# Half-tile tails, merged cross scores and new turns in a two-layer decoder kernel

## The chip, the cores and the metric

The kernel runs on one core of a Trainium2 chip. The metric is the time of one execution in microseconds (us), as the device takes it. TensorE (PE in the profile) multiplies, VectorE (DVE), ScalarE (ACT) and GpSimd (POOL) work on tiles, and SyncE (SP) issues DMAs.

## The reference, cut to what matters

Two decoder layers over x of 8 batches, 256 tokens and 256 features. Each layer is self attention, cross attention over 77 context tokens, and a mixture of experts, and each of the three ends in a residual and a layer norm.

```python
x = _layernorm(x + _L0_attn_ref(x, ...))        # gated linear attention, 4 heads
x = _layernorm(x + _L0_xattn_ref(x, ctx_768, ...))  # cross attention, 16 heads of 16
x = _layernorm(x + _L0_ffn_ref(x, ...))         # 8 experts, the best 2 of each token
x = _layernorm(x + _L1_attn_ref(x, ...))        # window of 128 to either side, 16 heads
x = _layernorm(x + _L1_xattn_ref(x, ctx_768, ...))  # cross attention, scores clipped
x = _layernorm(x + _L1_ffn_ref(x, ...))         # 8 experts with a capacity
```

Cross attention in the reference is

```python
att = jax.nn.softmax(jnp.einsum('blhd,bmhd->blmh', q, k) * scale, axis=2)
out = jnp.einsum('blmh,bmhd->blhd', att, v).reshape(b, l, d)
return jnp.einsum('bld,ed->ble', out, Wo) + bo
```

## The kernel before

The batches go in four pairs. Within a pair one batch is p0 and one is p1; each has its own buffers and four of the eight PSUM banks, so that one works while the other waits. What follows calls them layer 1 (the stages that `first_layer` lists: gated linear attention and cross attention X0) and layer 2 (`second_layer`: self attention S1 and cross attention X1). The experts stand between the layers and at the end, and don't take part in the change, apart from the early routing that is mixed into the last pair of each layer.

The work of a batch is a thread, a list of stages. A stage is a small function on one engine: `scores` on TensorE, `max` on VectorE, `exp` on ScalarE and so on. `in_turns` merges the threads of p0 and p1 into one list: it takes so many stages of p0, then so many of p1, by the numbers in `TURNS0`, `LAST0`, `TURNS1`, `LAST1` and `TURNS_HEAD`. `play` lets every engine walk through that one list and issue the stages that it owns. So each engine does its own stages in the order of the list, strictly one behind the other, and between engines only semaphores hold. Stages of different engines that stand side by side in a thread overlap; what matters is the order of the stages of one engine.

Attention goes in these steps. `scores` multiplies queries by keys (lines 1583 and 1591), `max` takes the negated row maxima (L874, L878), `split` turns them into bf16 (L886 to L890), `nmT` and `nmTe` turn them (L1604, L635). `ST` computes the scores again, transposed (L1630), and adds the maxima as shift rows (L1612); in X1, `clip` (L895) stands between the two and `shift` adds the rows. `exp` is on ScalarE (L645). Then comes the tail: `values` (L1658), `OT` copies the result (L649), `untr` turns it back (L1666), `norm` divides by the sums (L901, L903), `tout` turns it (L1673), `onT` copies it (L653), `wo` is the output product (L1680), and `res` adds the residual and starts the layer norm (L910, L833 to L840), whose power is on GpSimd (L1388). `final` is L846. A tail handles both 128-token tiles of the batch at once. In gated linear attention the last stages are `g_turn` (L1775), which needs the rows that GpSimd and ScalarE scaled, `g_yT` (L710), `g_wo` (L1783), `g_res` (L976) and `g_fin`.

A float32 product of one call leaves two matmul records in the trace. In cross scores a call has 77 columns, one head's keys; 16 calls, 32 records, make a unit of 128 queries, and four of them run in different row groups of the array.

`idle` (L1566) issues bf16 products that nobody reads, in counts given by the `IDLE` constants: 4 before the shift rows of p0's cross attention, 4 of 204 columns after p1's first unit of scores, 4 and 6 after the products that wait for a clip, 4 in p1's `g_turn` and 2 in each `route` of the pairs before the last. Outside the pairs are 50 before layer 2, 20 and 8 around the last experts, and 12 in each layer's last `turn_result`.

TensorE's order in a middle pair of layer 1, from the mix on:

```
g_mix:0 g_mix:1 k:0 g_turn:0 g_turn:1 g_wo:0 g_wo:1 k:1 v:0 turn:0 v:1 q:0 turn:1 q:1 scores.0:0 scores.0:1
scores.1:0 scores.1:1 nmT:0 ST.0:0 nmT:1 ST.0:1 ST.1:0 ST.1:1 values:0 values:1 untr:0 untr:1 tout:0 tout:1 wo:0 wo:1
```

(The number after the colon is the batch, p0 or p1.) VectorE's has `g_res:0 g_fin:0 g_res:1 g_fin:1`.

## Time and profile before

| what | us |
|---|---|
| median of 3 runs | 1130.51 |
| lowest and highest run | 1126.09, 1133.84 |
| the profiled execution's span, first to last instruction | 1131.2 |
| TensorE busy | 1010.0 (89%) |
| VectorE busy | 618.1 (55%) |
| ScalarE busy | 425.0 (38%) |
| GpSimd busy | 255.4 (23%) |

The profile gives the profiled execution by its span, and no time beside it; the span lies within the times of the runs. Layer 1's pairs fill the span from the start to some 380 us, the first experts follow to some 600, layer 2's pairs to some 1035, and the last experts end it. Busy shares are means over all of that.

### The profile page before, as it was taken

To read this page: it belongs to the slowest core of one execution; us is meant where nothing else is said; L and a number is where in the kernel's file an instruction comes from. 1 tells how busy PE (TensorE), PEld (TensorE's weight loads), DVE (VectorE), ACT (ScalarE), POOL (GpSimd) and SP (SyncE) were. 2 spreads that over 40 slices of the span, in tenths; PEclk is the share of its full clock that TensorE was granted. 3 is DMA by queue.
4 is the path that set the end of the run, shared out by engine and by line. 5 is a ranking of instruction groups with operands and counts; after the bars stand their busy time and mean duration, and the time that the engine had idled before them with its cause. 6 is when DMAs were issued, how large, how long until landed. Compare 5 with 4: busy or idle time off the path is not lost.

```text
span 1131.2 us, 20802 instructions
## 1 busy us (share of the span) xinstructions
PE 1010.0 (89%) x8612; PEld 719.1 (64%) x8612; DVE 618.1 (55%) x1398; ACT 425.0 (38%) x557; POOL 255.4 (23%) x282
## 2 busy tenths in 40 slices
PE   6889889999987899999998798879888987986997
PEld 3666566576575799997445465747565665654566
DVE  2653753662667564333334846675575668765443
ACT  1533533524433355555541254142416231541112
POOL 0310310120130233333322020231013110210662
PEclk9999999899897899999999899999999999997999
DMA  6013413211400691111113000200020010004447
GB/s 188 1 43 126 135 43 107 89 43 44 152 1 1 254 378 57 47 48 47 43 39 98 1 2 6 85 2 5 1 76 2 6 38 1 1 2 131 130 135 236
DMA packets 64237, 80.50 MB, mean 71 GB/s; under 512 B 12736, under 2 KB 57680, under 8 KB 63120
## 3 DMA queue, kind: packets, MB, share of 16 engines
q1 hardware_dynamic: 53392, 61.15, 16.3%
q0 software_dynamic: 5664, 15.47, 4.2%
q10 hardware_dynamic: 5088, 2.56, 0.9%
q8 instruction: 68, 1.11, 0.4%
q14 instruction: 25, 0.20, 0.1%
HBM read 46.13 MB, written 33.03 MB: 70 GB/s over the span
## 4 chain that ended last, share of the span: by engine, by line
PE 61%; DVE 17%; ACT 12%; issue 5%; DMA 2%; POOL 2%; SPq 0%; ACTq 0%; DVEq 0%; POOLq 0%
PE ps L1522 8%; PE ps L1857 7%; DVE sb_arena L874 6%; ACT sb_arena L645 6%; PE ps L1658 5%; PE ps L1680 4%; PE ps L1885 4%; PE ps L1868 3%; PE ps L1728 3%; PE ps L1783 3%; DVE sb_arena L878 3%; PE ps L1566 2%; PE ps L1995 2%; PE ps L1630 2%; PE ps L1905 2%
## 5 line engine op out<-in xcount | busy, mean ns | idle before, releaser
L645 ACT ACTIVATE sb_arena<-ps 77x2048 f32<-77x2048 f32 (+1 forms) x64 | 116.5, 1880 | 27.9 <-PE ps L1612 26.7
L1388 POOL TENSOR_TENSOR sb_arena<-sb_arena,sb_neghalf 128x2 f32<-128x2 f32 x40 | 28.7, 719 | 397.2 <-DVE sb_arena L840 397.2
L1522 PE MATMUL ps<-sb_arena,sb_wreg 128*128 128x256 f32 (+1 forms) x512 | 110.8, 365 | 6.8 <-issue 3.8
L1522 PEld LDWEIGHTS ps<-sb_arena,sb_wreg 128*128 128x128 f32 (+1 forms) x512 | 89.0, 195 | 23.7 <-issue 8.3
L1857 PE MATMUL ps<-sb_arena 128*128 128x128 f32 x800 | 100.2, 280 | 3.2 <-ACT sb_arena L757 2.3
L1630 PE MATMUL ps<-sb_arena 32*77 32x256 f32 (+1 forms) x1024 | 78.4, 424 | 25.8 <-ACT sb_arena L645 13.1
L1857 PEld LDWEIGHTS ps<-sb_arena 128*128 128x128 f32 x800 | 97.0, 196 | 5.2 <-ACT sb_arena L757 2.9
L757 ACT ACTIVATE sb_arena<-sb_arena 128x1024 f32 x72 | 76.0, 1057 | 16.8 <-issue 12.4
L1630 PEld LDWEIGHTS ps<-sb_arena 32*77 32x77 f32 (+1 forms) x1024 | 44.3, 177 | 46.1 <-ACT sb_arena L645 24.2
L874 DVE TENSOR_REDUCE sb_arena<-ps 128x8 f32<-128x2048 f32 x32 | 71.0, 2282 | 3.5 <-PE ps L1586 3.5
L1566 PE MATMUL ps<-sb_headrow,sb_identb 128*32 128x512 bf16 (+1 forms) x266 | 65.8, 385 | 1.4 <-DVE sb_arena L878 1.3
L1465 POOL DMA_INDIRECT outs<-sb_arena,sb_idx x36 | 35.5, 987 | 134.8 <-ACT sb_arena L743 134.8
L901 DVE RECIPROCAL sb_arena<-ps 128x32 f32<-128x32 f32 x24 | 8.6, 357 | 100.2 <-PE ps L1666 98.7
L635 ACT ACTIVATE sb_nmTb<-ps 128x256 bf16<-128x256 f32 x24 | 9.2, 383 | 143.5 <-PE ps L1604 143.5
L1658 PE MATMUL ps<-sb_arena,sb_va 77*32 77x256 f32 (+1 forms) x1024 | 58.5, 381 | 3.1 <-ACT sb_arena L645 2.5
L1728 PE MATMUL ps<-sb_wreg,sb_arena 128*128 128x512 f32 x128 | 60.7, 635 | 0.2 <-DVE sb_arena L926 0.2
L1409 POOL TENSOR_SCALAR_AFFINE_SELECT sb_arena<-sb_arena 128x512 f32<-128x512 f32 x48 | 29.6, 647 | 125.2 <-ACT sb_arena L645 125.2
L878 DVE TENSOR_REDUCE sb_arena<-ps 128x16 f32<-128x1232 f32 x32 | 45.4, 1438 | 21.1 <-PE ps L1591 21.0
L846 DVE TENSOR_SCALAR sb_arena<-sb_arena 128x256 f32<-128x256 f32 x80 | 39.2, 531 | 27.3 <-POOL sb_arena L1388 27.1
L1680 PE MATMUL ps<-sb_wreg,sb_arena 128*128 128x256 f32 x192 | 45.2, 384 | 5.7 <-ACT sb_arena L653 5.7
L1658 PEld LDWEIGHTS ps<-sb_arena,sb_va 77*32 77x32 f32 (+1 forms) x1024 | 31.2, 110 | 27.4 <-ACT sb_arena L645 8.7
L1583 PE MATMUL ps<-sb_arena 32*128 32x256 f32 x512 | 36.7, 400 | 13.2 <-DVE sb_arena L874 13.2
(285 smaller groups left out, 1886.9 us busy)
## 6 DMA issues: line engine op xcount, KB each, us to landing
sb_arena<-in_m_w SPq DMA_DIRECT2D x8, 1536.0 KB, 9.8
sent<-sb_xres SPq DMA_DIRECT2D x32, 256.0 KB, 2.6
sb_arena<-outs SPq DMA_DIRECT2D x16, 512.0 KB, 6.0
outs<-sb_zeros SPq DMA_DIRECT2D x4, 1664.0 KB, 9.7
sent<-sb_zeros SPq DMA_DIRECT2D x2, 2560.0 KB, 13.7
sb_arena<-in_m_w SPq DMA_DIRECT2D x16, 256.0 KB, 3.4
early<-sb_xres SPq DMA_DIRECT2D x12, 256.0 KB, 2.9
sb_arena<-in_xT SPq DMA_DIRECT2D x8, 256.0 KB, 3.2
```

Source lines behind the costliest of these rows:

```text
L645: nc.scalar.activation(dst, src, ACT.Exp).then_inc(S(f"h_PT{p}"), 1)
L757: nc.scalar.activation(arena[:, to:to + 1024], arena[:, bass.ds(blk * WORDS + 1024 * part, 1024)], ACT.Copy).then_inc(S(signal), 1)
L874: v.tensor_reduce(b.nm[:, :, u].rearrange("p (t r) -> p r t", t=NT), bank(p, 0, RT).rearrange("p r (t k) -> p r t k", t=NT), axis=AX.X, op ...
L878: v.tensor_reduce(b.nm[:, u * RT:(u + 1) * RT, :], bank(p, 0, RT)[:, :, 0:G * M].rearrange("p r (g k) -> p r g k", g=G), axis=AX.X, op=ALU ...
L1522: ins = mm(dst[:, m * cols:(m + 1) * cols], wt[0:rows, k, m * P:(m + 1) * P], src[0:rows, k, 0:cols], start=(k == 0), stop=(k == KC - 1))
L1566: ins = mm(bank(p, n)[IDLE:P, first:], identb[:, IDLE:P], headrow[:, :, :].rearrange("p g k -> p (g k)")[:, first:], start=True, stop=True ...
L1630: ins = mm(bank(p, r)[0:c.keys, a * L:(a + 1) * L], key, b.q[rows_of(r), u // 2 if c.selfattn else u, :], start=(a == 0), stop=False, skip ...
L1658: ins = mm(bank(p, 2 + g // 2)[rows_of(r), (g % 2) * L:(g % 2 + 1) * L], b.va[0:c.keys, kt, g * RT + r, :], b.PT[0:c.keys, g, first:first ...
L1680: ins = mm(bank(p, 3)[:, t * D:(t + 1) * D], bufs[p].onT[:, k, t * P:(t + 1) * P], W[f"{c.name}_wo"][:, k, :], start=(k == 0), stop=(k == ...
L1728: ins = mm(bank(p, 2 + t), b.xT[:, k, t * P:(t + 1) * P], W[wt][:, k, :], start=(k == 0), stop=(k == KC - 1))
L1857: ins = mm(to[:, m * P:(m + 1) * P], w[:, k, m * P:(m + 1) * P], slots0[j % 2].xT[:, k, :], start=(k == 0), stop=(k == KC - 1))
L1885: ins = mm(to[rows, :], slots0[j % 2].xT[:, k, rows], weights_of(c, blk, at + FH * k, FH, at + FH * k), start=(k == 0), stop=(k == KC - 1) ...
```

## The change

1. Tails in halves. `values` and `OT` are stages for two of the four head groups each; `untr`, `norm`, `tout`, `onT`, `wo` and `res` are stages for one 128-token tile each. The second tile's turned heads and its result go to banks of their own (`turned_bank`, `result_bank`).
2. Cross scores. One call multiplies 128 queries by the keys of two heads, 154 columns, so a unit has 8 calls in place of 16.
3. The unread products in the pairs go (six counts are 0). The 50, 20, 12 and 8 remain; the 12 of p0 now wait for its residual.
4. One list of turns for each layer in place of a list for each pair. In layer 1 every turn is one stage. In layer 2 it is a new list of some 500 numbers. The places of the early routing in the last pair change with it.
5. The early count moves from p0's bank to p1's, with its waits.

TensorE's order in a middle pair of layer 1 becomes

```
g_mix:0 g_mix:1 k:0 g_turn:1 g_turn:0 g_wo:1 g_wo:0 k:1 v:0 v:1 turn:0 turn:1 q:0 q:1 scores.0:0 scores.0:1
scores.1:0 scores.1:1 nmT:0 nmT:1 ST.0:0 ST.0:1 ST.1:0 ST.1:1 values.0:0 values.0:1 values.1:0 values.1:1
untr.0:0 untr.0:1 untr.1:0 untr.1:1 tout.0:0 tout.0:1 tout.1:0 tout.1:1 wo.0:0 wo.0:1 wo.1:0 wo.1:1
```

and VectorE's has `g_res:0 g_res:1 g_fin:0 g_fin:1`. In layer 2 the middle pairs keep the order of before but for neighbours that change places; the tail of S1 becomes

```
values.0:0 values.1:0 values.0:1 values.1:1 untr.0:0 untr.1:0 untr.0:1 tout.0:0 untr.1:1 tout.1:0 tout.0:1 wo.0:0 wo.1:0 tout.1:1 wo.0:1 wo.1:1
```

```diff
-IDLE, IDLE_SPLIT, IDLE_CLIP = 96, 4, (4, 6)
-IDLE_TURN, IDLE_LAYERS, IDLE_ROWS, IDLE_SCORES, IDLE_RESULT, IDLE_MIXED, IDLE_ROUTE = 4, 50, 20, 4, 12, 8, 2
+IDLE, IDLE_SPLIT, IDLE_CLIP = 96, 0, (0, 0)
+IDLE_TURN, IDLE_LAYERS, IDLE_ROWS, IDLE_SCORES, IDLE_RESULT, IDLE_MIXED, IDLE_ROUTE = 0, 50, 20, 0, 12, 8, 0
...
-    for t in range(NT):
-        out += [("scores", c, t), ("max", c, t)]
+    for i in range(c.score_units):
+        out += [("scores", c, i), ("max", c, i)]
...
-    return [(n, c) for n in ("values", "OT", "untr", "norm", "tout", "onT", "wo", "res", "rstd", "final")]
+    out = []
+    for i in range(2):
+        out += [("values", c, i), ("OT", c, i)]
+    for n in (("untr", "norm"), ("tout", "onT"), ("wo", "res")):
+        for t in range(NT):
+            out += [(x, c, t) for x in n]
+    return out + [("rstd", c), ("final", c)]
...
-def in_turns(n, threads, turns, extra):
+def in_turns(threads, turns, extra):
 
     out, at = [], [0, 0]
     for i, count in enumerate(turns):
         p = i % 2
-        for stage, m in threads[p][at[p]:at[p] + count]:
-            if m < PAIRS:
-                out.append((stage, p, m))
-            out += [((e,), 0, n) for e in extra.get((p, *stage), [])]
+        for stage, n in threads[p][at[p]:at[p] + count]:
+            out.append((stage, p, n))
+            out += [((e,), 0, n) for e in extra.get((p, n, *stage), [])]
         at[p] += count
-    assert at == [len(t) for t in threads]
+    assert at == [len(t) for t in threads], (at, [len(t) for t in threads])
...
-TURNS0 = (3, 3, 4, 2, 3, 4, 2, 3, 4, 2, 3, 4, 5, 7, 4, 1, 2, 4, 4, 4, 2, 1, 4, 4, 1, 2, 2, 2, 2, 2, 2, 2, 2, 1, 2, 7, 6, 3, 5, 4)
-TURNS1 = (3, 3, 2, 2, 1, 1, 2, 2, 5, 5, 5, 5, 2, 2, 2, 2, 2, 2, 3, 3, 2, 1, 3, 4, 1, 5, 6, 2, 2, 3, 3, 2, 3, 1, 3, 5, 3, 3, 1, 1, 3, 3, 2, 1, 2, 3, 8, 3, 3, 5, 4, 7, 4, 4)
-LAST0 = (2, 2, 2, 2, 6, 6, 2, 2, 3, 2, 6, 5, 5, 1, 2, 1, 3, 8, 3, 1, 2, 5, 5, 6, 2, 2, 3, 2, 2, 2, 7, 5, 4, 7, 3, 3)
-LAST1 = (3, 3, 2, 2, 2, 2, 1, 1, 5, 5, 5, 4, 1, 2, 2, 2, 2, 2, 1, 1, 3, 3, 6, 1, 1, 4, 2, 1, 2, 2, 2, 3, 4, 4, 1, 1, 4, 3, 1, 4, 3, 3, 2, 2, 2, 2, 2, 1, 1, 2, 3, 2, 3, 4, 6, 6, 8, 8)
-TURNS_HEAD = (3, 2, 3, 3, 2, 1, 1, 2, 2, 3)
+TURNS0 = (1,) * 560
+TURNS1 = (4, 2, 1, 1, 4, 1, 1, 1, 1, 6, 1, 1, 1, 1, 1, 1, 2, 2, 1, 1, 2, 2, 5, 1, 1, 3, 2, 2, 1, 2, 1, 1, 1, 1, 1, 1, 1, 2, 2, 2, 3, 2, 1, 1, 2, 1,
...
+def whole_thread(head, thread, p):
+
+    return head + [(stage, m) for n in range(PAIRS) for stage, m in thread(p, n) if m < PAIRS]
...
+EXTRA0 = {(1, LAST, "g_sp"): ["choose"], (1, LAST, "g_mix"): ["count"], (1, LAST, "g_y"): ["counts", "rank"],
+          (1, LAST, "split", X0): ["hots", "table"], (0, LAST, "tout", X0, 1): ["place"], (0, LAST, "onT", X0, 1): ["raw"],
+          (0, LAST, "wo", X0, 1): ["turned"], (1, LAST, "norm", X0, 1): ["index"], (0, LAST, "rstd", X0): ["first"],
+          (1, LAST, "final", X0): ["blocks"], (1, LAST, "store"): ["gather"]}
+EXTRA1 = {(0, 3, "kz", S1): ["choose"], (1, 3, "va", S1): ["count", "counts"], (0, 3, "values", S1, 0): ["rank"], (0, 3, "values", S1, 1): ["hots"],
+          (0, 3, "rstd", X1): ["place"]}
...
+    head = of_pair(0, "g_keys", "g_low", "g_decay", "g_z")
+    return in_turns([whole_thread(head, first_thread, p) for p in range(2)], TURNS0, EXTRA0)
...
+        def turned_bank(p, t):
+
+            return bank(p, 1 if t else 2)[:, 0:KC * P].rearrange("p (k q) -> p k q", k=KC)
+
+        def result_bank(p, t):
+
+            return bank(p, 2 if t else 3)[:, 0:D]
...
-            sp.wait_ge(S("h_res0"), X0.at(PAIRS))
+            sp.wait_ge(S("h_res0"), NT * X0.at(PAIRS))
...
-            def heads(p, n, c):
-                act.wait_ge(S(f"h_OT_done{p}"), c.at(n) + 1)
-                nc.scalar.activation(bufs[p].OT, bank(p, 2, 2), ACT.Copy).then_inc(S(f"h_OT{p}"), 1)
-
-            def onT(p, n, c):
-                act.wait_ge(S(f"h_onT_done{p}"), c.at(n) + 1)
-                nc.scalar.activation(bufs[p].onT, halves(bank(p, 2)), ACT.Copy).then_inc(S(f"h_onT{p}"), 1)
+            def heads(p, n, c, i):
+                act.wait_ge(S(f"h_OT_done{p}"), 2 * c.at(n) + i + 1)
+                nc.scalar.activation(bufs[p].OT[:, 2 * i:2 * i + 2, :], halves(bank(p, 2 + i)), ACT.Copy).then_inc(S(f"h_OT{p}"), 1)
+
+            def onT(p, n, c, t):
+                rows = slice(t * P, (t + 1) * P)
+                act.wait_ge(S(f"h_onT_done{p}"), NT * c.at(n) + t + 1)
+                nc.scalar.activation(bufs[p].onT[:, :, rows], turned_bank(p, t), ACT.Copy).then_inc(S(f"h_onT{p}"), 1)
...
+            def norm(p, n, c, t):
+                b = bufs[p]
+                dve.wait_ge(S(f"h_O{p}"), NT * c.at(n) + t + 1)
+                o = bank(p, t).rearrange("p (h x) -> p h x", x=2 * DH)
+                v.reciprocal(b.rec[:, t, :], o[:, :, DH]).then_inc(S(f"h_on{p}"), 1)
+                dve.wait_ge(S(f"h_on{p}"), 2 * (NT * c.at(n) + t) + 1)
+                v.tensor_tensor(b.on[:, t, :].rearrange("p (h x) -> p h x", h=H), o[:, :, 0:DH],
+                                b.rec[:, t, :].unsqueeze(2).broadcast_to([P, H, DH]), ALU.mult).then_inc(S(f"h_on{p}"), 1)
+
+            def residual(p, n, c, t):
+                b = bufs[p]
+                dve.wait_ge(S(f"h_wo{p}"), NT * c.at(n) + t + 1)
+                if t == 0:
+                    dve.wait_ge(S(f"h_xb{p}"), c.at(n) + 1)
+                v.tensor_tensor(b.res[:, t, :], result_bank(p, t), b.xb[:, t, :], ALU.add).then_inc(S(f"h_res{p}"), 1)
+                dve.wait_ge(S(f"h_res{p}"), NT * c.at(n) + t + 1)
+                ins = v.bn_stats(b.st1 if t else b.st0, b.res[:, t, :])
+                if t + 1 == NT:
+                    ins.then_inc(S(f"h_moments{p}"), 1)
+                    moments("h", p, c.at(n))
...
-                    for g in range(G):
+                    for k in range(KC):
                         for r in range(RT):
-                            ins = mm(bank(p, r)[:, g * M:(g + 1) * M], b.q[rows_of(r), g // 2, u * P:(u + 1) * P], kz[rows_of(r), g // 2, g % 2, :],
-                                     start=(g == 0), stop=True, skip_group_check=True)
-                    if p == 1 and u == 0:
-                        ins = idle(p, IDLE_SCORES, 0, G * M)
+                            ins = mm(bank(p, r)[:, 2 * k * M:2 * (k + 1) * M], b.q[rows_of(r), k, u * P:(u + 1) * P],
+                                     kz[rows_of(r), k, :, :].rearrange("p a m -> p (a m)"), start=(k == 0), stop=True, skip_group_check=True)
...
+            def values(p, n, c, i):
+                b = bufs[p]
+                if i == 0:
+                    pe.wait_ge(S(f"h_PT{p}"), c.exps_at(n) + c.exp_units)
+                for g in (2 * i, 2 * i + 1):
...
+            def untranspose(p, n, c, t):
+                if t == 0:
+                    pe.wait_ge(S(f"h_OT{p}"), 2 * (c.at(n) + 1))
+                for g in range(G):
+                    ins = tr(bank(p, t)[:, g * P:(g + 1) * P], bufs[p].OT[:, g, t * P:(t + 1) * P], ident[:, :])
...
+            def turn_out(p, n, c, t):
+                pe.wait_ge(S(f"h_on{p}"), 2 * (NT * c.at(n) + t + 1))
                 for k in range(KC):
-                    for t in range(NT):
-                        ins = tr(bank(p, 2)[:, k * L + t * P:k * L + (t + 1) * P], bufs[p].on[:, t, k * P:(k + 1) * P], ident[:, :])
+                    ins = tr(turned_bank(p, t)[:, k, :], bufs[p].on[:, t, k * P:(k + 1) * P], ident[:, :])
...
+            def project_out(p, n, c, t):
+                pe.wait_ge(S(f"h_onT{p}"), NT * c.at(n) + t + 1)
+                for k in range(KC):
+                    ins = mm(result_bank(p, t), bufs[p].onT[:, k, t * P:(t + 1) * P], W[f"{c.name}_wo"][:, k, :],
+                             start=(k == 0), stop=(k == KC - 1))
...
             def turn_result(p, n, c):
                 if n + 1 == PAIRS and p == 0:
+                    pe.wait_ge(S(f"h_res{p}"), NT * (c.at(n) + 1))
...
             def gla_keys(p, n):
                 b = bufs[p]
                 pe.wait_ge(S(f"a_in{p}"), 64 * (n + 1))
+                if n:
+                    pe.wait_ge(S(f"h_res{p}"), NT * X0.at(n))
```

## Rows read from the trace of the kernel before

**Rows 1.** The page, chain that ended last, by engine

```profile
PE 61%; DVE 17%; ACT 12%; issue 5%; DMA 2%; POOL 2%; SPq 0%; ACTq 0%; DVEq 0%; POOLq 0%
```

**Rows 2.** Windows of core 0: start:end, length, busy PE PEld DVE ACT POOL, clock, DMA, GB/s

```profile
111.36:198.10 86.74, 79.35 (x646) 56.39 (x646) 44.24 (x90) 35.31 (x52) 15.56 (x14) 1.00 0.31 100
...
730.70:833.94 103.24, 90.09 (x1024) 62.31 (x1024) 64.65 (x112) 36.84 (x40) 17.68 (x24) 1.00 0.08 23
...
785.60:805.40 19.80, 17.07 (x261) 9.24 (x263) 14.90 (x10) 7.32 (x8) 0.00 (x0) 1.00 0.01 2
...
135.35:142.04 6.69, 4.24 (x30) 2.99 (x29) 3.66 (x4) 4.49 (x10) 5.27 (x4) 1.00 0.00 0
```

**Rows 3.** The same window, the unread products of line 1566 alone

```profile
785.60:805.40 19.80, 6.57 (x28) 2.20 (x28) 1.00 0.01 2
```

**Rows 4.** Timeline of TensorE, layer 1: start, duration, line, tiles, count, wait

```profile
140.94 1.09 PE L1775 MATMUL ps<-sb_ident,sb_arena 128*128 128x128 f32 x8 [0.80 <-POOL sb_arena L1456]
...
142.04 7.20 PE L1783 MATMUL ps<-sb_wreg,sb_arena 128*128 128x256 f32 x32
...
149.08 1.01 PE L1522 MATMUL ps<-sb_arena,sb_wreg 96*128 96x77 f32 x8
...
157.12 2.13 PE L1591 MATMUL ps<-sb_arena 32*128 32x77 f32 x64
...
179.22 3.63 PE L1680 MATMUL ps<-sb_wreg,sb_arena 128*128 128x256 f32 x16
...
194.81 0.60 PE L1566 MATMUL ps<-sb_headrow,sb_identb 128*32 128x512 bf16 x2
```

**Rows 5.** Timeline of VectorE, the same pair

```profile
145.81 0.69 DVE L976 TENSOR_TENSOR sb_arena<-ps,sb_arena 128x512 f32<-128x512 f32 x1 [6.63 <-PE ps L1783]
...
147.61 0.17 DVE L840 TENSOR_SCALAR sb_arena<-sb_arena 128x2 f32<-128x2 f32 x1
...
158.32 4.21 DVE L878 TENSOR_REDUCE sb_arena<-ps 128x16 f32<-128x1232 f32 x3 [1.99 <-PE ps L1591]
```

**Rows 6.** Timeline of ScalarE, the same pair

```profile
140.98 2.11 ACT L710 ACTIVATE sb_arena<-ps 128x1024 f32<-128x1024 f32 x2
...
166.18 7.15 ACT L645 ACTIVATE sb_arena<-ps 77x2048 f32<-77x2048 f32 x4
```

**Rows 7.** Timeline of TensorE, layer 2

```profile
785.65 2.13 PE L1591 MATMUL ps<-sb_arena 32*128 32x77 f32 x64
...
791.12 1.04 PE L1566 MATMUL ps<-sb_headrow,sb_identb 128*32 128x512 bf16 x4 [0.22 <-DVE sb_arena L878]
...
792.85 1.10 PE L1630 MATMUL ps<-sb_arena 32*77 32x256 f32 x16 [0.47 <-ACT sb_nmTb L635]
...
802.96 0.42 PE L1612 MATMUL ps<-sb_nmTb,sb_headrow 32*77 32x256 bf16 x8
...
812.63 1.99 PE L1680 MATMUL ps<-sb_wreg,sb_arena 128*128 128x256 f32 x8 [0.69 <-ACT sb_arena L653]
...
816.23 1.99 PE L1680 MATMUL ps<-sb_wreg,sb_arena 128*128 128x256 f32 x8 [0.74 <-ACT sb_arena L653]
```

**Rows 8.** Timeline of VectorE, layer 2, the clips

```profile
794.02 4.49 DVE L895 TENSOR_SCALAR ps<-ps 77x2048 f32<-77x2048 f32 x2 [1.18 <-PE ps L1630]
...
800.21 4.49 DVE L895 TENSOR_SCALAR ps<-ps 77x2048 f32<-77x2048 f32 x2 [1.70 <-PE ps L1630]
```

**Rows 9.** Windows of core 0 at a lower clock

```profile
346.00:348.00 2.00, 2.00 (x16) 0.76 (x12) 1.39 (x1) 0.00 (x0) 0.00 (x0) 0.50 0.00 0
...
644.00:646.00 2.00, 1.56 (x16) 1.36 (x20) 1.93 (x6) 1.97 (x3) 0.00 (x0) 0.64 0.00 0
```

**Rows 10.** Timeline of TensorE in the window of 346

```profile
349.16 2.00 PE L1630 MATMUL ps<-sb_arena 32*77 32x256 f32 x16 [0.47 <-ACT sb_nmTb L635]
```

**Rows 11.** Timeline of TensorE, the early choice in layer 2

```profile
933.16 0.43 PE L1797 MATMUL ps<-sb_masked,sb_causal 128*128 128x96 f32 x2 [1.10 <-DVE sb_masked L1036]
```

**Rows 12.** Timeline of VectorE, p0's last residual in layer 1

```profile
371.42 0.68 DVE L910 TENSOR_TENSOR sb_arena<-ps,sb_arena 128x512 f32<-128x512 f32 x1
```

More of the change, by code:

```diff
@@ L207, in second_thread, with second_layer @@
         of_pair(n + 1, *self_head(S1)[3:])
-def second_head():
-    return in_turns(0, [of_pair(0, "mix", "mix_rstd", "mix_fin", *self_head(S1))] * 2, TURNS_HEAD, {})
-def second_layer(n):
-    extra = {}
-    if n + 1 == PAIRS:
-        extra = {(1, "exp", S1, 0): ["rank", "hots"], (1, "wo", X1): ["place"]}
-    if n + 2 == PAIRS:
-        extra = {(1, "kz", S1): ["choose"], (0, "v", S1): ["count", "counts"]}
-    return in_turns(n, [second_thread(p, n) for p in range(2)], LAST1 if n + 1 == PAIRS else TURNS1, extra)
+def second_layer():
+    head = of_pair(0, "mix", "mix_rstd", "mix_fin", *self_head(S1))
+    return in_turns([whole_thread(head, second_thread, p) for p in range(2)], TURNS1, EXTRA1)
 def play(order, stages):
@@ L777, in _ @@
             act.wait_ge(S("rescaled"), 3)
-            play(head1, stages)
-            for order in order1:
-                play(order, second)
+            play(order1, second)
             picks(3, 4)
@@ L1309, in _ @@
             scale_bias(["s1_bq", "x1_bq"], "rescaled")
-            play(head1, stages)
-            for order in order1:
-                play(order, stages | routing(1))
+            play(order1, stages | routing(1))
             choose_late(1)
@@ L1475, in store1 @@
                     unread(p)
-            play(head1, stages)
-            for order in order1:
-                play(order, stages | {"store": lambda p, n: store1(p, n)})
+            play(order1, stages | {"store": lambda p, n: store1(p, n)})
             def gather1(e):
```

108 lines of the change are left out of this document (36 added, 72 removed), and 9 rows, old and new, of the table TURNS1.

## Prediction

> **What bounds the kernel now.** I read the chain that ended last first: TensorE holds 61% of it, VectorE 17%, ScalarE 12% [rows 1]. The windows then show how full TensorE is. One pair of batches takes 86.7 us in layer 1 and 103.2 us in layer 2, and TensorE has no matmul for 7.4 and 13.2 us of them (span of the window less TensorE's busy time) [rows 2]. So a saving counts only where TensorE, or the engine that it waits for, comes last. The timelines by engine show four kinds of stretch: the dense ones, where TensorE sets the pace; the maxima and the clips, where VectorE does (a clip takes 2.25 us, four stand in a pair [rows 8]); the exponentials, where ScalarE does (1.8 us each [rows 6]); and the joints between them, where the hand-written order decides.
>
> The last view is the windows with the granted clock. In the maxima and clips of cross attention, 785.6 to 805.4, TensorE is busy for 17.07 of 19.8 us at full clock [rows 2], but 6.57 us of that are unread products [rows 3]. The reader should keep both numbers.
>
> The profiled span is 1131.2 us; the median of the runs is 1130.5. I carry the sum on the span and take the 0.7 off at the end.
>
> **Layer 2, a pair at full clock.** Laid side by side engine by engine, the new order has nearly the old sequence: the two batches still alternate, p0 slightly ahead. New are the halves.
> - Self attention's tail. TensorE waits some 0.6 us there for the normalisation of the second batch, as in cross attention; with halves the other tile's turns fill that. -0.6 us.
> - Merged score product. 64 records of 77 columns take 2.13 us, about 1.03 us for a unit of 32 [rows 7]. A unit becomes 16 records of 154 columns. The floor is half, 0.5 us; the ceiling is no saving, if a record costs by its columns. Sixteen records of 256 columns take about 1.0 us [rows 7], 60 ns each against 32 ns for 77 columns; on the line between them 154 columns cost 44 ns, 0.7 us a unit. Only the first unit lies on the path, since VectorE needs 1.4 us for each maximum [rows 5]. -0.3 us (0 to -0.5).
> - Split idle. Four unread products start at 791.12, when p0's last maximum is there, and the shift rows must wait 0.97 us for them [rows 7]. What they are to cover is one small cast, some 0.2 us by the 0.17 us of a small operation [rows 5]. -0.75 us.
> - Clip idles. The second pair of clips starts at 800.21 and its first half ends at 802.45 [rows 8], but the shift rows start at 802.96 [rows 7], behind four unread products: 0.45 us. At the first clip I estimate 0.2. -0.65 us.
> - Cross attention's tail. TensorE waits 0.69 and 0.74 us for ScalarE's copy of the turned heads [rows 7]. In halves, one tile's turn hides the other's copy. A tail gets five more operations on ScalarE and VectorE, each at least the 0.17 us of a small one [rows 5]; both engines are idle beside it. -1.1 us.
>
> The Trainium skill, TensorEngine Tiling (Array Packing), section Instruction Overhead, says that a matmul has some 60 cycles of overhead and is no cheaper below 60 columns. By it both 77 and 154 columns lie above the floor, a unit would take what it took, and 0.3 us would be lost again in each of eight cross attentions, 2.4 us in all. The rows speak against it: 256 columns cost less than twice what 77 cost.
>
> Together -3.4 us, -10.2 for three pairs. The last pair has no follow-up work in its tail, and its 12 unread products now wait for the residual: -2.6. Its early routing sits better: choosing the experts makes TensorE wait 1.10 us between two value products [rows 11], and in the new order all projections run during that chain: -1.0. The head of the layer: -0.5, as the first batch's query product fills the wait for the second batch. **Layer 2: -14.3 us** (-9 to -18).
>
> **Layer 1, a pair at full clock.** Here the strict turns move work across the joints.
> - After the gated mix p1's turn now comes ahead of p0's (the key product stands before it in p0's thread). TensorE still waits there for GpSimd's rows of p1, until 140.94 [rows 4]. Then come p1's turn, p0's turn, and p1's output product waits for ScalarE's 1.0 us copy of p1's turned rows, which starts at about 142.1. Today p0's copy runs from 140.98 [rows 6] and the product starts at 142.04 [rows 4]. It now starts at 143.2: +1.1 us.
> - VectorE's order changes from residual p0, final p0, residual p1, final p1 to both residuals, then both finals, and p0's residual comes behind the second output product. A residual with its statistics takes 1.97 us, 145.81 to 147.78 [rows 5]. The second product ends 7.0 us after the start of the first, at 150.2 [rows 4]; p0's input is normalised at 150.2 + 1.97 + 1.9 + 0.75 = 154.9. TensorE has one key and two value products in between, some 0.87 us each, to 152.8: it waits 2.1 us. Both queries follow both turns, and the scores start at 160.4 instead of 157.12 [rows 4]: 3.3 us late, the 1.1 included.
> - Maxima to exponentials: -0.3 (merged) and -0.75 (idles), against +1.0, since p0's shift rows now stand behind the last maximum of p1 and behind p1's own rows in all three engines. 0.
> - Tail: the first half of p1's values stands before the second half of p0's and waits for p1's last exponential, 1.8 us less the 0.9 of p0's half [rows 6]. The output products start at 180.1 instead of 179.22 [rows 4]: +0.9.
> - The router's two groups of two unread products lay on a full TensorE, 0.43 us from the start of one to the next work [rows 4]: -0.9.
>
> That is +3.3 us a pair, +9.9 for three. In the last pair VectorE's one-hots and tables hold the chain anyway; only its end counts, where SyncE's queue holds the load of the experts' weights until p0's residual is done. Today that residual runs from 371.42 to 372.1 [rows 12]. In strict turns its second half comes behind four halves of normalisation, the index and two other halves of the residual, and ends at about 373.1: +1.0. **Layer 1: +10.9 us** (+4 to +15). The halves lie beside TensorE's work here too; without that cover 24 tails of five small operations would cost 20 us.
>
> Both layers: 10.9 - 14.3 = -3.4 us.
>
> **The clock.** The unread products do more than fill. Within the paired work I count seven falls to the lower level (0.5, that is 1.2 GHz), each behind thin work on TensorE; two windows of them are shown [rows 9]. The one of 346 lasted 13 us, behind maxima with a wait of 1.5 us, though TensorE was full again in most of it. The one of 644 stands at the joint between maxima and exponentials, and the same joint fell in two of four pairs. At the lower level 16 records of products take 2.00 us instead of 1.10 [rows 7, 10]. Without idles and with merged scores the clip stretch [rows 2] has 17.07 - 6.57 - 1.3 = 9.2 us of work in some 17.5 us, 53%, about what that joint has. So I expect falls in two of the four pairs of layer 2. Each costs two products at +0.9, two groups of shift rows at +0.25 and 1.8 us of the values: 4.1 us, 8.2 in all. In layer 1 the wait before the output product, 4.24 us busy in 6.69 [rows 2] with 1 us of idles in it, should fall in two more pairs, at an estimated 1.2 us each: 2.4. Together +10.6. The Trainium skill, TensorE: Matmul & The Clock Gate, section What's actually happening, calls the lower level the default, which activity releases; the rows agree as far as every fall here follows thin work.
>
> Sum: 1131.2 - 3.4 + 10.6 = 1138.4 on the span, **1137.7 us** against the median.
>
> **The rivals.**
> 1. *The clock holds* (0.28). What is left are matmuls still, and the self scores run warm with half a microsecond of wait in every 2.2. Then 1130.5 - 3.4 = 1127 (1121 to 1132).
> 2. *The clock falls in every thin stretch* (0.22), the slower side: four pairs of layer 2 and three cross attentions of layer 1 at 4.1, four joints at 1.2, 33.5 us less 3.4. It passes 1% with the fourth fall of the 4.1 kind. For it: 53% busy. Against it: two of four at the joint. 1147 to 1161.
> 3. *The strict turns are paid for* (0.12): p0's residual gets through sooner than my row by row sum, and the value half waits less. Then layer 1 costs 4 instead of 10.9 and the clock holds: 1120; 1116 if layer 2 gives its 18.
> 4. *The new order does not act* (0.03): every engine plays its stages from one list, so the order can't fail to take place; only the merged product can save nothing, +2.4.
>
> My forecast (0.35) has 1132 to 1147 as its own range. For 8 in 10 the range takes in rival 1 and the lower half of rival 2: 1118 to 1154.
>
> **Chances.** 1% is 11 us, about what a measurement of this kernel can tell from no change. Below 1119: rival 3 and an edge of rival 1, 0.15. Above 1142: rival 2 and over a third of my case, 0.35. Between them 0.50.
>
> **What would show it.** In a pair of layer 1, a wait of 2 us before the cross attention's input is turned, and a period of 90 instead of 86.7 us. In layer 2, no waits in the tails, clips 1.6 us nearer to the self tail, and periods below 100 us where the clock is 1.00. In the clock's windows, falls in the clip stretch. I am wrong if the clock shows none there, or if the scores of layer 1 start as early as now.

## The result, and the profile after

The changed kernel takes 1171.02 us (median of 4, 1165.77 to 1177.97) against 1129.35 us: ratio 1.0376, 95% interval 1.0327 to 1.0425, slower. Forecast were 1137.7 us and a range to 1154. The profiled execution has a span of 1164.0 us; it was the fastest of the four, so the traces show 32.8 of the some 42 us.

The cores' view has span and mean granted clock of TensorE, first the changed kernel, then the kernel before:

```profile
core 0: 1164.0 us, clock 0.919
```

```profile
core 0: 1131.2 us, clock 0.967
```

At the lower of the two levels, 0.5, TensorE spends an estimated (1 - 0.919) x 2 x 1164.0 = 189 us in place of 75. Its busy time hardly changed (1003.0 and 1010.0 us), although the unread products are gone. The page's line of TensorE and its chain that ended last [rows 1], which gained in TensorE and VectorE:

```profile
PE 1003.0 (86%) x7928; PEld 727.0 (62%) x7928; DVE 628.2 (54%) x1470; ACT 432.2 (37%) x605; POOL 256.7 (22%) x282
...
PE 63%; DVE 19%; ACT 7%; issue 5%; DMA 3%; POOL 2%; SPq 0%; ACTq 0%; DVEq 0%; POOLq 0%
```

The windows of the changed kernel (start:end, length, busy PE, PEld, DVE, ACT, POOL, clock, DMA share, GB/s) answer to [rows 2]: a pair of each layer, the maxima and clips, then the joint from the gated mix to its output product. The last three cut one clip stretch and what follows into the part ahead of a fall, the fall, and the part behind it.

```profile
120.20:215.73 95.53, 81.62 (x567) 59.24 (x566) 44.51 (x96) 35.99 (x56) 15.65 (x14) 0.91 0.28 90
757.19:862.81 105.62, 88.23 (x932) 62.23 (x933) 67.57 (x125) 38.06 (x48) 18.11 (x24) 0.92 0.07 22
811.41:831.31 19.90, 11.33 (x173) 6.41 (x176) 14.93 (x10) 7.76 (x8) 0.00 (x0) 0.85 0.01 2
144.03:152.99 8.96, 4.46 (x25) 4.25 (x25) 3.75 (x4) 4.60 (x10) 5.35 (x4) 0.81 0.00 0
...
819.00:825.00 6.00, 2.82 (x48) 1.42 (x48) 4.58 (x3) 3.43 (x3) 0.00 (x0) 1.00 0.00 0
825.00:842.00 17.00, 14.37 (x117) 8.82 (x118) 6.48 (x9) 7.11 (x8) 0.00 (x0) 0.51 0.01 1
842.00:850.00 8.00, 7.57 (x41) 6.14 (x40) 5.73 (x21) 2.21 (x6) 1.95 (x3) 0.98 0.00 2
```

The reader should see two things. A pair of layer 1 is 8.8 us longer, one of layer 2 is 2.4. And the clip stretch comes first at full clock with TensorE thin (2.82 of 6.0 us busy); then the clock is at 0.51 for 17 us, though TensorE is busy for 14.37 of them.

The timeline of TensorE, layer 1, beside [rows 4]:

```profile
149.71 3.45 PE L1794 MATMUL ps<-sb_ident,sb_arena 128*128 128x128 f32 x16 [3.43 <-POOL sb_arena L1476]
...
164.66 0.66 PE L1534 MATMUL ps<-sb_ident,sb_arena 128*128 128x128 f32 x4 [1.98 <-DVE sb_arena L859]
166.42 1.11 PE L1534 MATMUL ps<-sb_ident,sb_arena 128*128 128x128 f32 x4 [1.11 <-DVE sb_arena L859]
167.32 4.87 PE L1540 MATMUL ps<-sb_arena,sb_wreg 128*128 128x256 f32 x16
...
178.95 0.52 PE L1621 MATMUL ps<-sb_identb,sb_nmb 128*128 128x128 bf16 x4 [2.29 <-DVE sb_nmb L903]
...
189.27 4.37 PE L1676 MATMUL ps<-sb_arena,sb_va 77*32 77x256 f32 x48 [0.69 <-ACT sb_arena L654]
193.57 3.67 PE L1684 MATMUL ps<-sb_ident,sb_arena 128*128 128x128 f32 x16
```

The waits are where the steps put them, 3.43 us before the turns, 1.98 before p0's input (2.1 foreseen), 0.69 in the values. Behind nearly each of them stands work that is longer than its records take at full clock: 16 turns in 3.45 us, 16 in 3.67, where 8 took 1.09 [rows 4].

The same view for layer 2, beside [rows 7]:

```profile
817.53 1.10 PE L1647 MATMUL ps<-sb_arena 32*77 32x256 f32 x16 [0.47 <-ACT sb_nmTb L644]
...
823.25 0.42 PE L1629 MATMUL ps<-sb_nmTb,sb_headrow 32*77 32x256 bf16 x8 [1.78 <-DVE ps L908]
...
825.64 2.00 PE L1647 MATMUL ps<-sb_arena 32*77 32x256 f32 x16 [1.09 <-ACT sb_arena L654]
...
830.65 7.06 PE L1676 MATMUL ps<-sb_arena,sb_va 77*32 77x256 f32 x64
```

From the scores to the second pass of products it is 6.12 us in place of 7.20, the saving of 1.05 that was foreseen. From there to the output product it is 24.43 in place of 19.78: the 64 value records take 7.06 us, and 3.73 at full clock (in a run below).

A landmark parts the loss: VectorE's first maxima of layer 2 start 23.4 us later, by its timeline before and after. The experts took the same: from their first turn to these maxima it is 243.3 us, and 243.7 before. So layer 1 lost 23.4 us, and layer 2 9.4. Foreseen were 13.3 (10.9 + 2.4) and -6.1 (-14.3 + 8.2). (The second line is from a view that ends before the seventh maximum.)

```profile
625.06 15.47 DVE L874 TENSOR_REDUCE sb_arena<-ps 128x8 f32<-128x2048 f32 x7 [0.86 <-PE ps L1586]
```

```profile
648.49 13.28 DVE L887 TENSOR_REDUCE sb_arena<-ps 128x8 f32<-128x2048 f32 x6 [0.86 <-PE ps L1605]
```

### The profile page after: what moved, and what is told of

The parts are those of the page before. It is cut to its first block, busy times and chain, and to the rows that moved or that the text cites. A ratio compares the mean times of both kernels' runs of the same rounds, so it can differ in the third digit from the quotient of the medians.

```text
span 1164.0 us, 19568 instructions
## 1 busy us (share of the span) xinstructions
PE 1003.0 (86%) x7928; PEld 727.0 (62%) x7928; DVE 628.2 (54%) x1470; ACT 432.2 (37%) x605; POOL 256.7 (22%) x282
## 3 DMA queue, kind: packets, MB, share of 16 engines
q8 instruction: 63, 1.03, 0.4%
## 4 chain that ended last, share of the span: by engine, by line
PE 63%; DVE 19%; ACT 7%; issue 5%; DMA 3%; POOL 2%; SPq 0%; ACTq 0%; DVEq 0%; POOLq 0%
PE ps L1540 8%; PE ps L1876 7%; PE ps L1676 6%; DVE sb_arena L887 6%; ACT sb_arena L654 5%; PE ps L1747 5%; PE ps L1904 3%; PE ps L1647 3%; PE ps L1887 3%; DVE sb_arena L891 3%; PE ps L1696 3%; DVE ps L908 3%; PE ps L1802 2%; PE ps L1684 2%; PE ps L2012 2%
## 5 line engine op out<-in xcount | busy, mean ns | idle before, releaser
L1540 PE MATMUL ps<-sb_arena,sb_wreg 128*128 128x256 f32 (+1 forms) x512 | 113.7, 375 | 5.5 <-issue 3.8
L1647 PE MATMUL ps<-sb_arena 32*77 32x256 f32 (+1 forms) x1024 | 88.9, 471 | 21.1 <-ACT sb_arena L654 11.7
L1540 PEld LDWEIGHTS ps<-sb_arena,sb_wreg 128*128 128x128 f32 (+1 forms) x512 | 93.1, 203 | 22.4 <-issue 8.7
L767 ACT ACTIVATE sb_arena<-sb_arena 128x1024 f32 x72 | 76.0, 1057 | 17.9 <-issue 13.9
L1676 PE MATMUL ps<-sb_arena,sb_va 77*32 77x256 f32 (+1 forms) x1024 | 78.2, 471 | 5.1 <-ACT sb_arena L654 4.5
L914 DVE RECIPROCAL sb_arena<-ps 128x16 f32<-128x16 f32 x48 | 12.3, 256 | 125.4 <-PE ps L1684 122.7
L1647 PEld LDWEIGHTS ps<-sb_arena 32*77 32x77 f32 (+1 forms) x1024 | 48.7, 193 | 43.8 <-ACT sb_arena L654 22.8
L1676 PEld LDWEIGHTS ps<-sb_arena,sb_va 77*32 77x32 f32 (+1 forms) x1024 | 38.0, 131 | 39.5 <-issue 16.9
L1747 PE MATMUL ps<-sb_wreg,sb_arena 128*128 128x512 f32 x128 | 55.9, 595 | 0.2 <-DVE sb_arena L944 0.2
L1887 PE MATMUL ps<-sb_arena 128*128 128x256 f32 x200 | 47.4, 380 | 0.0
L633 ACT ACTIVATE sb_arena<-ps 128x512 f32<-128x512 f32 x24 | 14.1, 596 | 89.6 <-PE ps L1534 89.6
## 6 DMA issues: line engine op xcount, KB each, us to landing
sent<-sb_zeros SPq DMA_DIRECT2D x2, 2560.0 KB, 14.3
```

The lines of the kernel that those rows point to most:

```text
L767: nc.scalar.activation(arena[:, to:to + 1024], arena[:, bass.ds(blk * WORDS + 1024 * part, 1024)], ACT.Copy).then_inc(S(signal), 1)
L1540: ins = mm(dst[:, m * cols:(m + 1) * cols], wt[0:rows, k, m * P:(m + 1) * P], src[0:rows, k, 0:cols], start=(k == 0), stop=(k == KC - 1))
L1647: ins = mm(bank(p, r)[0:c.keys, a * L:(a + 1) * L], key, b.q[rows_of(r), u // 2 if c.selfattn else u, :], start=(a == 0), stop=False, skip ...
L1676: ins = mm(bank(p, 2 + i)[rows_of(r), (g % 2) * L:(g % 2 + 1) * L], b.va[0:c.keys, kt, g * RT + r, :], b.PT[0:c.keys, g, first:first + L], ...
L1747: ins = mm(bank(p, 2 + t), b.xT[:, k, t * P:(t + 1) * P], W[wt][:, k, :], start=(k == 0), stop=(k == KC - 1))
L1887: ins = mm(bank(1, 3)[:, 0:D], slots0[p].hT[:, m, :], work["w3"][:, m, :], start=(m == 0), stop=(m == MC - 1))
```

## The experiments

The first four make a square with the two kernels: unread products or none, strict or old turns in layer 1.

```diff
-IDLE, IDLE_SPLIT, IDLE_CLIP = 96, 0, (0, 0)
-IDLE_TURN, ..., IDLE_SCORES, ..., IDLE_ROUTE = 0, ..., 0, ..., 0
+IDLE, IDLE_SPLIT, IDLE_CLIP = 96, 4, (4, 6)
+IDLE_TURN, ..., IDLE_SCORES, ..., IDLE_ROUTE = 4, ..., 4, ..., 2
```

**idles_back** is the changed kernel with this.

> The changed kernel with the six counts of unread products as before (4, (4, 6), 4, 4, 2), everything else changed. Theory, the unread products held the clock: the mean granted clock returns from 0.919 to about 0.965, and only the order and the halves are left. My sum without the clock was -3.4 us, and the unread products on the path were worth 11.3 of gain in it (1.4 in each of four pairs of layer 2, 0.75 and 0.9 in layer 1), so 1130.5 - 3.4 + 11.3 = 1138 us (1133 to 1144). Rival, the halves and the strict turns make the stretches thin by themselves: the falls of the clock stay and the time stays above 1158 us.

1140.47 us (ratio to the kernel before 1.0085, 1.0051 to 1.0118), within the theory's range. The square below shows that luck had a part in it: the strict order costs 25.7 us where the sum has 16.6, the rest of the change gains 15.7 where it has 8.7 (16.6 - 8.7 = 11.3 - 3.4), and the two errors nearly cancel.

**before_no_idles** is the kernel before with the same lines the other way.

> The kernel before with the same six counts at 0, nothing else changed. Theory, the unread products held the clock: they save 11.3 us on the path, and the clock takes back what the changed kernel lost by it, 1171 less 1127 (my sum without the clock) = 44 us: 1130.5 - 11.3 + 44 = 1163 us (1152 to 1172), granted clock about 0.92. Rival, the order and the halves cost the time: the products were in the way, and the time is 1119 to 1135 us with a clock above 0.95.

1165.05 us (1.0295, 1.025 to 1.034), clock 0.906, within the theory's range. The old order with 16 score calls and whole tails loses 35 us by this alone. Its window from the second pass of products to the output product in layer 2:

```profile
807.23:833.31 26.08, 20.66 (x183) 11.69 (x183) 11.78 (x10) 10.51 (x8) 0.00 (x0) 0.57 0.01 1
```

19.78 us with the unread products. So the long fall needs neither halves nor new turns.

**old_order** (no unread products) and **idles_old_order** (with them) give layer 1 the old order of every engine, halves side by side; only the early count keeps its new place:

```diff
-TURNS0 = (1,) * 560
+TURNS0 = (1, 1, 1, 1, 1, 1, 1, 1, 3, 3, 4, 2, 3, 4, 2, 3, 4, 2, 3, 4, 5, 7, 4, 1, 2, 4, 4, 4, 2, 1, 4, 4, 1, 2, 2, 2,
...
```

> The changed kernel without unread products, but TURNS0 is a list that gives layer 1 the order of before, with the two halves of each tail stage side by side. Theory, the order costs what its waits cost and no more: 3.3 us a pair for three pairs, 1171 - 9.9 = 1161 us (1156 to 1167), and the cross attentions of layer 1 show falls of the clock as now. Rival, the waits of the strict order (3.4, 2.0 and 2.3 us in a pair of layer 1) are what brings the clock down: the falls of layer 1 go back to the six of before, another 10 us or more are gained, 1150 us or less.

> Both at once: the six counts of unread products as before, and layer 1 in the order of before. What is left of the change are the halves, the merged score product and the order of layer 2. Theory: 1138 - 9.9 = 1128 us (1122 to 1133), and layer 2 has periods some 2 us shorter than the 103.2 and 105 us of before. Rival, the halves cost time by their extra operations: 1138 us or more.

1146.28 us (1.0148, 1.0107 to 1.019) and 1114.76 us (0.9863, 0.9832 to 0.9894). The theory missed in both: the strict order costs not 10 but 25 us. In the first the rival's number held, but not its mechanism, as is shown below the table.

| us, median | strict turns | old turns | difference |
|---|---|---|---|
| no unread products | 1171.0 | 1146.3 | 24.7 |
| unread products | 1140.5 | 1114.8 | 25.7 |
| difference | 30.5 | 31.5 | |

The two differences add up with hardly anything between them, but the order doesn't cost by the same means in both columns. The estimate of time at the lower level, (1 - clock) x 2 x span, is as a median over each kernel's runs 203 us (strict) and 191 (old) without unread products, 77 and 47 with them. So without them the old order is 24.7 us faster with about as much time at the lower level. Windows of old_order, for a pair of layer 1, from the mix to the first output product, and from there to the scores:

```profile
114.20:206.04 91.84, 82.66 (x566) 58.66 (x566) 44.93 (x96) 35.89 (x56) 15.56 (x14) 0.89 0.29 93
...
140.28:148.02 7.74, 5.21 (x29) 4.50 (x27) 4.02 (x6) 4.49 (x10) 5.35 (x4) 0.68 0.00 0
148.02:163.95 15.93, 15.24 (x73) 12.47 (x73) 8.69 (x28) 2.94 (x5) 3.54 (x4) 0.94 0.24 74
```

In the changed kernel the three are 95.53 us at 0.91, 9.26 at 0.82 and 19.14 at 0.91: longer at a higher clock. TensorE is idle for 13.9 us of that pair (95.53 - 81.62) and for 9.2 of this one. There the order costs by its waits. With unread products, where the old order keeps its clock, the strict one spends 30 us more at the lower level. By the values, 7.06 us for 3.73, work there takes about twice its time, so by this estimate the clock makes up at most 15 of the 25.7 us, and the waits the rest.

The kernel with unread products and the old order, 1114.8 us, is 1.4% faster than the kernel before. Its windows (a pair of layer 2; layer 1 from the mix to the first output product; layer 2 from the second pass of products to the output product) and a line of its timeline of TensorE:

```profile
722.00:822.45 100.45, 88.08 (x960) 60.47 (x961) 67.26 (x125) 37.78 (x48) 18.11 (x24) 1.00 0.08 24
...
136.53:143.60 7.07, 4.62 (x33) 3.18 (x31) 4.01 (x6) 4.49 (x10) 5.35 (x4) 1.00 0.00 0
...
783.11:801.67 18.56, 16.92 (x202) 8.60 (x203) 10.58 (x10) 10.35 (x10) 0.00 (x0) 1.00 0.01 2
```

```profile
795.61 3.73 PE L1681 MATMUL ps<-sb_arena,sb_va 77*32 77x256 f32 x64 [0.18 <-ACT sb_arena L657]
```

**turn_first** and **res_order** put back one part each of the strict order; of TensorE's and VectorE's order in the middle pairs of layer 1 only this changes (in turn_first ScalarE's two copies between turn and product change places too; in the last pair a few stages beside them move):

```
turn_first:  g_turn:1 g_turn:0 g_wo:1 g_wo:0    (for g_turn:0 g_turn:1 g_wo:0 g_wo:1)
res_order:   g_res:0 g_res:1 g_fin:0 g_fin:1    (for g_res:0 g_fin:0 g_res:1 g_fin:1)
```

> From the kernel with unread products and the old order of layer 1 (1114.8 us), one part of the strict turns put back: p1's turn, copy and output product after the gated mix stand ahead of p0's, in all four pairs; VectorE's order is the old one. Theory: p1's product starts 1.1 us later, p0's residual must wait for the second product, and the thin stretch before the product brings the clock down once in a pair (1.2 us): 3.5 to 4.5 us a pair, 1130 us (1124 to 1136). Rival, the strict turns cost by the order of the residuals: 1119 us or less.

> From the same kernel, the other part alone: VectorE does both residuals and then both final steps (with their power on GpSimd), TensorE's turns stay old. Theory: p0's final step comes behind p1's residual, which is 1.2 us later than now, and little of it is covered: 1.2 us a pair, 1120 us (1117 to 1123). Rival, this order is the costly one (the 2.0 and 1.1 us of wait before the two turns in the strict kernel): 1126 us or more.

1142.58 us (1.0125, 1.0079 to 1.017) and 1125.06 us (0.9964, 0.9944 to 0.9985). The first costs 27.8 us, more than either account gave, and as much as all strict turns together. Its windows, from the mix to the first output product and on to the scores, and VectorE's timeline:

```profile
143.96:153.31 9.35, 5.82 (x32) 4.85 (x31) 4.01 (x6) 4.60 (x10) 5.35 (x4) 0.82 0.00 0
153.31:171.47 18.16, 14.75 (x75) 11.60 (x73) 8.64 (x28) 2.94 (x5) 3.54 (x4) 1.00 0.22 65
```

```profile
160.45 0.69 DVE L997 TENSOR_TENSOR sb_arena<-ps,sb_arena 128x512 f32<-128x512 f32 x1 [12.29 <-PE ps L1807]
```

p0's residual waits for the second output product, 12.29 us against 6.63 [rows 5]. That is 3.1 us more from product to scores (18.16 against 15.08), at full clock; the first window is 2.3 longer, with a fall in it. Together 5.4 us in this pair, 22 if all four are alike, and more falls elsewhere. Both this kernel and the strict one put p1's turn ahead and leave p0's residual first; no kernel was run that exchanges the residuals too, so whether it is the combination that costs stays open. In res_order the stretch from product to scores takes 16.19, 1.1 us more, as expected; the four of them are 4.4 of its 10.3 us, which are twice what was expected. The rest goes with the clock, 0.969 in place of 0.979, (0.031 x 1123.9 - 0.021 x 1113.0) x 2 = 23 us more at the lower level. The two parts, 27.8 and 10.3 us, don't add up to the 25.7 of the whole strict order, so neither is a share of it.

**no_clip**, **no_split** and **clip_only** ask which unread products matter. The first two start from idles_old_order, the third from the changed kernel.

```diff
 no_clip:   IDLE_CLIP = (0, 0)
 no_split:  IDLE_SPLIT = 0, IDLE_SCORES = 0
 clip_only: IDLE_CLIP = (4, 6), the other five 0
```

> From the same kernel, the 4 and 6 unread products around each clip left out, the others kept. Theory: these hold the clock in layer 2. Without them the stretch from the clips to the output product takes what it takes in the changed kernel, 24.7 in place of 18.6 us, in four pairs: 1139 us (1130 to 1145). Rival, the 4 products before the shift rows and the 4 in the scores hold it: without those of the clips 0.65 us a pair is saved, 1112 us.

> From the same kernel, the 4 unread products before the shift rows and the 4 after the first score unit left out, those of the clips kept. Theory: they lie on the path and cost 0.75 us in each of eight cross attentions, and the clock stays: 1109 us (1106 to 1112). Rival, they hold the clock as well: 1120 us or more, with falls in the cross attentions of layer 1, which have no others.

> The changed kernel with the 4 and 6 unread products around each clip and no others. Theory: the cross attentions of layer 2 lose the long falls (clips to output product 24.7 us now, 18.6 with all unread products); without those of the scores a short fall stays as in no_split, 21.2: 3.5 us in each of four pairs, 1157 us (1151 to 1162), layer 1 as it is. Rival, layer 2's falls come from the order and the halves: 1166 us or more.

1137.08 us (1.0067, 1.0043 to 1.0092), 1126.89 us (0.9987, 0.9964 to 1.0009) and 1152.58 us (1.0229, 1.0181 to 1.0277). no_clip is the theory's: 22 us for four clip stretches. In no_split the theory fell and the rival held: scores to products is 6.12 us in place of 6.87, the 0.75 that they cost, but the clock takes back more, in layer 1 too (from 163 to 170 us, behind the maxima of cross attention, it is 0.52). clip_only lies in its expected range. Windows from the second pass of products to the output product, no_clip, no_split and clip_only:

```profile
789.40:813.83 24.43, 18.47 (x183) 10.86 (x183) 11.31 (x11) 10.65 (x10) 0.00 (x0) 0.65 0.00 1
```

```profile
788.39:809.67 21.28, 19.73 (x202) 9.39 (x203) 11.31 (x12) 10.31 (x10) 0.00 (x0) 0.85 0.01 2
```

```profile
811.49:832.94 21.45, 19.90 (x202) 9.46 (x203) 11.31 (x12) 10.31 (x10) 0.00 (x0) 0.84 0.00 1
```

With both kinds it is 18.56 us at clock 1.00. So each kind holds a part: without the clips' the clock is low from 797 to the output product (0.50), without the others' it falls at the start of the stretch (0.51 from 788 to 795) and is 1.00 for the rest. clip_only gives 18 of the 30.5 us back, layer 1 as it was.

**single_heads** issues 16 calls of one head again.

> From the kernel with unread products and the old order of layer 1 (1114.8 us), the cross scores again as 16 calls of 77 columns in place of 8 of 154, nothing else. Theory (a record costs by columns only in part): the first unit is on the path, its maxima start 0.3 us later, in eight cross attentions, 1117.2 us (1116 to 1119). Rival, the merged product thins TensorE's work and costs clock: 1113 us or less. Rival from a price by columns alone: 1114.8.

1122.06 us (0.9925, 0.9902 to 0.9948), 7.3 more, above the expected 1116 to 1119. From scores to products it is 7.20 in place of 6.87 us, 0.33 us in each of eight, 2.6: the expected price. A part of the rest is a fall in layer 1's last pair that both the kernel before [rows 9] and this one have, and the merged one hasn't; windows of 13 us of that stretch, single_heads and idles_old_order:

```profile
346.00:359.00 13.00, 10.58 (x108) 5.74 (x104) 11.47 (x54) 4.40 (x4) 0.00 (x0) 0.51 0.01 2
```

```profile
344.00:357.00 13.00, 8.45 (x142) 5.35 (x146) 12.48 (x65) 8.86 (x8) 0.00 (x0) 1.00 0.01 3
```

The merged calls gave TensorE less to do and kept it at full clock there; why, these runs don't tell. That fall isn't the whole rest: from the first scores of the last pair to its last output product it is 33.82 us against 32.00, 1.8 of the 8.6 between the profiled spans. Where the others come from wasn't followed.

**old_layer2** and **old_layer2_b** give layer 2 the order of before too. The first had a wait of my making.

> From the same kernel, TURNS1 is a list that gives layer 2 the order of before too, the two halves of each tail stage side by side (the early routing keeps its new places). What is then left of the change are halves and merged scores. Theory, the interleaved halves and the new places of the last pair gain: 1.0 us a pair and 1.4 more in the last are lost, 1120 us (1117 to 1123). Rival, the halves gain by themselves, in whatever order: 1113 to 1116 us.

> The kernel of old_layer2, but ScalarE copies p0's value halves after p1's last exponential, as before. Theory, the new order of layer 2 is worth something by itself, but little: without that wait the self tail takes 11.0 us or less in place of 13.3, three pairs give back 2.3 each, 1124 to 1126 us; the rest to 1114.8 is order, most of it in the last pair and in falls of the clock. Rival, the halves gain by themselves: 1114 to 1118 us.

1131.98 us (1.0012, 0.9993 to 1.0032) and 1120.86 us (0.9938, 0.9912 to 0.9964). In the first, ScalarE's list had p0's second value half ahead of p1's last exponential (L652 exp, L656 the copy), and TensorE paid:

```profile
767.40 0.60 ACT L656 ACTIVATE sb_arena<-ps 128x512 f32<-128x512 f32 x1 [1.13 <-PE ps L1676]
767.89 1.87 ACT L652 ACTIVATE sb_arena<-ps 128x2048 f32<-128x2048 f32 x1
...
769.82 3.66 PE L1676 MATMUL ps<-sb_arena,sb_va 128*32 128x256 f32 x64 [2.48 <-ACT sb_arena L652]
```

One stage in the wrong place in three pairs cost 11 us. Against the second, the new list of layer 2 is worth 6.1 us and halves with merged scores 8.7 (1129.6 to 1120.9), most of it by the merged scores if their 7.3 hold here too. 1120.9 lies between the two expectations, so both missed.

**split_2**, **more_idles** and **route_4** tune the counts of the fastest kernel (IDLE_SPLIT = 2; IDLE_TURN = 8 and IDLE_ROUTE = 4; IDLE_ROUTE = 4).

> From the same kernel, 2 unread products in place of 4 before the shift rows of cross attention. Theory: the first two cover the cast for which the shift rows wait anyhow, the other two lie on the path, 0.45 us in each of eight: 1111.2 us (1109 to 1113), if two are enough for the clock. Rival, they are not: the falls behind the maxima come as in the kernel without them, 1118 us or more.

> From the same kernel, 8 unread products in place of 4 before p1's turn of the gated mix and 4 in place of 2 before each routing product. Six falls of the clock are left in this kernel before 400 us, at 110, 200, 316, 360 and 376. Theory (falls come from thin work, wherever it is): the products cost 0.45 us twice and some 0.5 us once in a pair, 1.4 us, 5 in all, and take away the falls behind them, 2 to 3 of them at 1.7: 1116 us (1113 to 1120). Rival, their places are full enough already: 1120 us and the falls as they are.

> The fastest kernel so far (1114.8 us) with 4 unread products in place of 2 before each routing product of the first three pairs. Theory: they cost 0.5 us a pair and take away the two falls behind them, as in more_idles, where the stretch from routing to the end of the mix took 21.2 in place of 22.5 us: -0.8 us a pair, 1112.5 us (1110 to 1115). Rival, the falls only move elsewhere: 1116 us or more.

1117.38 us (0.9896, 0.9859 to 0.9934), 1117.58 us (0.9887, 0.9867 to 0.9907) and 1115.54 us (0.9882, 0.9855 to 0.9911). None can be told from 1114.8 with certainty, and the theories' gains are not there. split_2 has falls behind the maxima, as its rival said (0.52 from 165 to 172 us, where idles_old_order has 1.00). In route_4 the 32 records behind the routing (128x512) take 13.98 us in place of 15.68, as hoped, and a fall stands a little later instead, at the joint of the mix, 138 us. With 8 unread products the joint of the mix got longer by more than they take, 8.39 for 7.07, with a fall in it:

```profile
138.53:146.92 8.39, 6.75 (x36) 4.50 (x35) 4.00 (x6) 4.49 (x10) 5.35 (x4) 0.80 0.00 0
```

## Why the prediction was wrong

The forecast went the right way and was far too small: 1137.7 us for a measured 1171.0. The step that failed is the price of the clock, +10.6, and behind it the price of the strict order in layer 1. Two more landmarks of VectorE part them, the first maxima of layer 2 in old_order and in idles_back (the slowest of its five runs, 1145.5 us of span):

```profile
628.05 15.48 DVE L890 TENSOR_REDUCE sb_arena<-ps 128x8 f32<-128x2048 f32 x7 [0.86 <-PE ps L1608]
```

```profile
650.98 15.48 DVE L887 TENSOR_REDUCE sb_arena<-ps 128x8 f32<-128x2048 f32 x7 [0.86 <-PE ps L1605]
```

- *The clock, +10.6.* The step that failed, in layer 2 above all. "Falls in two of the four pairs of layer 2, 4.1 us each": there was one in each of four, and in the first and the last pair a second. And each was priced too low: the price had 1.8 us more for the values, and they took 3.3 more (7.06 against 3.73), and the fall went on to the output product, 17 us in all, though TensorE had been full for 11. From products to output product that is 24.43 against 18.56 us, 5.9. From the first maxima to the end, layer 2 and the last experts take 515.5 us in the changed kernel and 494.5 in idles_back, which has the same order with unread products: +21.0. Foreseen were 8.2 for the clock less 5.6 for the products on the path, +2.6. In layer 1, "in two more pairs, at 1.2 us each": a pair has some 17 us at the lower level ((1 - 0.91) x 2 x 95.53), in four places, 149, 166, 180 and 190 us in the pair that is shown. But the old order has as much of it, so this is the price of the missing unread products and not of the strict turns.
- *Layer 1, order, +10.9.* The waits stand where they were put, and with their sizes: the residuals' wait 1.98 us (2.1), the values' wait 0.69 (0.9). The strict order's own terms in this step (1.1, 2.2, 1.0 and 0.9 a pair, 1.0 in the last) make 16.6 us. By the landmark it costs layer 1 20.4 us (648.49 against 628.05), by the medians of the runs 24.7. What is left of layer 1's 23.4, 3.0 us, is what halves, merged scores and the missing unread products come to; foreseen were -3.3 (10.9 - 16.6 + 2.4). So of the 10.1 us by which layer 1 was missed, 3.8 are the order and 6.3 the rest, the clock in it.
- *Layer 2, order and halves, -14.3.* Right in its parts, and the sum a little short. Scores to products 7.20 to 6.12 (foreseen -1.05, found -1.08); cross tail, in idles_back, 19.78 to 18.56 from products to output product (foreseen -1.1, found -1.2); split idles 0.75 found by leaving them out; merged scores 0.33 a cross attention (0.3). Without the 5.6 us for unread products 8.7 were foreseen, and idles_back has 494.5 us there for 506.1 before, 11.6 less. With +21.0 for +2.6 that makes the 15.5 us by which layer 2 was missed.
- *Clip idles, -0.65 a pair.* At the first clip 0.22 us: from the first product of the second pass to the third group of products it is 5.97 us in the changed kernel (817.53 to 823.50), still at full clock, and 6.19 in idles_old_order. The 0.45 at the second clip wasn't seen: no run without these products kept its clock to there.
- *Rival 2*, that the clock falls in every thin stretch, came nearest, and its 1147 to 1161 was too low since it used the same two prices. The range stopped in its middle. What spoke against it, that two of four joints fell, was read as a chance for each stretch; but in the kernel before, the clip stretches had never been tried without their cover. They were known at 86% busy and were to be at 53%, and only the rows of thin stretches could speak of that.
- *Rival 1* is out by the granted clock, 0.919, and by before_no_idles. *Rival 3* is out by the wait of 1.98 us and by old_order. *Rival 4* is out by old_order and old_layer2_b, where a changed list changes the time, and by single_heads, where the merged product saves what it was to save.

One premise of the clock's part doesn't hold. It says that each fall in the kernel before stands behind thin work. By two more of its windows the one at 197 doesn't:

```profile
183.00:197.00 14.00, 14.00 (x70) 10.08 (x68) 5.02 (x16) 2.01 (x5) 2.68 (x4) 1.00 0.59 191
...
197.00:204.00 7.00, 7.00 (x15) 3.60 (x16) 2.07 (x5) 3.44 (x5) 0.00 (x0) 0.53 1.04 348
```

TensorE is busy for all of the 14 us before it. The last of that work are small products: of 16 rows (L1721), 4 unread ones, and the router's of 8 columns (L1701). A busy share alone, the 53% of the forecast or the 86% of before, doesn't tell where the clock falls.

The Trainium skill, TensorE: Matmul & The Clock Gate, section What's actually happening, calls the lower level the default, which activity releases. These runs agree in so far as the time at the lower level went from 77 to 203 us and from 47 to 191 when the unread products were taken out; the fall at 197, behind 14 us without a gap, is one that the rule in this form doesn't tell. By the Trainium skill, TensorEngine Tiling (Array Packing), section Instruction Overhead, read as the prediction read it, a call of 77 columns lies above the floor and the merged scores were to save nothing; 7.20 against 6.87 us says that they save a third of a unit's 1.03 us.
